# A two-layer graph network on one core: three weight masks and the low parts of x on VectorE in stage one, two more adjacency tiles split

## The reference

```python
node = x @ W1                                  # 4096 x 16
hw = einsum('nc,kcf->nkf', x, W2)              # 16 products of 128 x 128
x0 = einsum('nk,nkf->nf', node, hw)
x1 = layernorm(x + relu(adj @ x0 + node @ b0))

sens = exp(-(1/adj - 1)**2 / (2 * 0.5**2))
weights = where(adj < 1, sens, 0)              # 4096 x 4096
out = layernorm(x1 + weights @ (x1 @ W + B))
```

## Time and profile before

| | |
|---|---|
| median of 3 runs | 548.31 us (548.08 to 548.40) |
| the profiled execution: its time, its span | 548.46 us, 546.6 us |
| TensorE, VectorE, ScalarE, GpSimd busy | 99%, 92%, 91%, 15% of the span |
| granted TensorE clock | full in all slices but the last, 0.99 there |

### The profile page before, as it was taken

How to read it: one execution, slowest core, us unless ns; L and a number is a source line. 1 busy time by engine, 2 the same in 40 slices (tenths; PEclk the granted TensorE clock), 3 DMA queues, 4 the chain that set the end, 5 groups by cost and what they waited for, 6 DMA issues and landing times.

```text
span 546.6 us, 5236 instructions
## 1 busy us (share of the span) xinstructions
PE 541.2 (99%) x1800; PEld 332.0 (61%) x1800; DVE 504.6 (92%) x561; ACT 498.2 (91%) x449; POOL 83.3 (15%) x76
## 2 busy tenths in 40 slices
PE   9999999999999999999999999999999999999996
PEld 8888888655655565556555655565556556554444
DVE  5767777899999999999999999999999999999887
ACT  4778888669999999999999998999899899999994
POOL 1789989500000000000000000000000000000000
PEclk9999999999999999999999999999999999999999
DMA  5894000199998988888888898898988886870003
GB/s 165 321 424 173 27 2 0 31 367 422 414 360 300 339 335 315 303 330 314 334 306 314 321 349 305 312 317 320 327 315 308 316 330 236 322 267 1 0 19 135
DMA packets 23130, 142.05 MB, mean 260 GB/s; under 512 B 2720, under 2 KB 3264, under 8 KB 6720
## 3 DMA queue, kind: packets, MB, share of 16 engines
q1 hardware_dynamic: 22960, 141.46, 69.7%
q10 hardware_dynamic: 144, 0.26, 0.2%
HBM read 139.62 MB, written 2.10 MB: 259 GB/s over the span
## 4 chain that ended last, share of the span: by engine, by line
PE 99%; ACT 0%; DVE 0%; issue 0%; POOL 0%; ACTq 0%; POOLq 0%
PE kept_ps L526 20%; PE l_ps L526 18%; PE acc_ps L475 14%; PE acc_ps L464 7%; PE acc_ps L465 7%; PE acc_ps L466 7%; PE hw_ps L434 6%; PE hw_ps L440 5%; PE hw_ps L437 5%; PE acc_ps L526 2%; PE acc_ps L412 1%; PE var_ps L507 1%; PE acc_ps L481 1%; PE hw_ps L554 1%; PE acc_ps L536 0%; PE kept_ps L536 0%
## 5 line engine op out<-in xcount | busy, mean ns | idle before, releaser
L935 DVE SCALAR_TENSOR_TENSOR wt_pair<-wt_pair 128x2048 f32<-128x2048 f32 x60 | 136.9, 2283 | 1.3 <-DMA wt_pair<-adjT_dram 1.3
L642 ACT ACTIVATE wt_pair<-wt_pair 128x4096 f32<-128x4096 f32 (+1 forms) x33 | 108.9, 3300 | 11.7 <-DVE wt_pair L935 11.7
L647 ACT ACTIVATE wt_pair<-wt_pair 128x4096 f32<-128x4096 f32 (+1 forms) x33 | 109.1, 3307 | 0.5
L526 PE MATMUL kept_ps<-wt_pair,msg 128*128 128x512 f32 x240 | 107.9, 592 | 0.0
L923 DVE TENSOR_TENSOR row_lo<-rows,adj_hi 128x2048 fp32r<-128x2048 f32 x42 | 96.3, 2292 | 1.4
L526 PE MATMUL l_ps<-wt_pair,msg 128*128 128x512 f32 x216 | 97.1, 592 | 0.0
L626 ACT ACTIVATE prods<-hw_ps,node 128x128 f32<-128x128 f32 x256 | 73.1, 373 | 19.1 <-PE hw_ps L440 17.5
L890 DVE SCALAR_TENSOR_TENSOR part_acc<-hw_ps,node,part_acc 128x128 f32<-128x128 f32 x224 | 60.8, 343 | 20.7 <-PE hw_ps L440 20.7
L475 PE MATMUL acc_ps<-rows,x 128*128 128x512 f32 x176 | 78.8, 592 | 0.0
L464 PE MATMUL acc_ps<-adj_hi,x_hi 128*128 128x512 f32 x168 | 75.5, 449 | 0.0
L526 PEld LDWEIGHTS kept_ps<-wt_pair,msg 128*128 128x128 f32 x240 | 45.4, 190 | 49.3 <-issue 47.8
(11 more groups left out here) (122 smaller groups left out, 603.4 us busy)
## 6 DMA issues: line engine op xcount, KB each, us to landing
rows<-adjT_dram SPq DMA_DIRECT2D x68, 1024.0 KB, 4.9
wt_pair<-adjT_dram SPq DMA_DIRECT2D x60, 1024.0 KB, 4.8
x_in<-xT_dram SPq DMA_DIRECT2D x8, 256.0 KB, 3.6
x_row<-xT_dram SPq DMA_DIRECT2D x8, 256.0 KB, 5.1
outT_dram<-sumT SPq DMA_DIRECT2D x7, 256.0 KB, 2.0
W_in<-W_dram SPq DMA_DIRECT2D x3, 256.0 KB, 4.8
W_in<-W_dram ACTq DMA_DIRECT2D x1, 256.0 KB, 3.7
outT_dram<-sumT SPq DMA_DIRECT2D x2, 128.0 KB, 1.9
```

The lines of the kernel that those rows point to most:

```text
L526: mm = pe.matmul(out, msg[:, c % 2, k, :], wt[t][:, k, :], start=(first and k == 0), stop=(last and k == CH - 1))
L642: act.activation(w, w, ACT.Ln, bias=TINY).then_inc(ln_made, 1)
L647: act.activation(w, w, ACT.Exp, scale=-1.0).then_inc(inv_made, 1)
L935: dve.scalar_tensor_tensor(out=w, in0=w, scalar=1.0, in1=w, op0=ALU.is_lt, op1=ALU.mult).then_inc(made, 1)
```

## The change

- Row tiles 14 (row 1, block 6) and 62 (row 7, block 6) are split too; 44 tiles are now. Since no block is split in some early row and unsplit in the last ones any more, the low parts of x0 all lie in place of x0, the separate `x0_apart` is gone, and three remainders wait for the unsplit tiles of rows 0 and 1 to be done.
- In stage one the low part of the next block of x is made by VectorE, between its pairs 1 and 2, and no longer by GpSimd.
- The masks of weight tiles 0, 1 and 2 are made by VectorE in stage one, behind blocks 2, 4 and 6.
- The first six weight tiles are loaded ahead of the first five row tiles.
- The written-out orders of VectorE and ScalarE in stage two are new in many places; on ScalarE the rounding of the last block of x0 stands behind the first Ln and Exp of tile 0.

```diff
-SPLIT = (1, 3, 4, 5, 6, 7)
-SPLIT_FIRST = ((3, 5, 7), (1, 3, 5, 7))
...
+SPLIT_IN_ROW = ((3, 5, 7), (1, 3, 5, 6, 7)) + 6 * ((1, 3, 4, 5, 6, 7),)
...
+MASKS_AFTER = (2, 4, 6)
...
+            for t in range(WT_RING - LATE_SLOTS):
+                load_wt(t)
             for i in range(ROW_RING):
                 load_row_tile(i)
-            for t in range(WT_RING - LATE_SLOTS):
-                load_wt(t)
...
-            round_x0(NB - 1)
             take_ln(0)
             take_inverse(0)
+            round_x0(NB - 1)
             take_square(0)
...
+            def remainder_of_x(g):
+                s = g % 2
+                dve.wait_ge(x_hi_made, g + 1)
+                dve.tensor_tensor(x_lo[:, s, :], x_in[:, s, :], x_hi[:, s, :], ALU.subtract).then_inc(x_lo_made, 1)
 
             def sum_over_k(g):
                 s = g % 2
                 dve.wait_ge(node_copied, g + 1)
                 for q in range(QUARTERS):
+                    if q == QUARTERS // 2 and g + 1 < NB:
+                        remainder_of_x(g + 1)
                     dve.wait_ge(hw_made[0], g * GROUPS + 2 * q + 2)
...
+                if g not in LO_APART:
+
+                    at_least(dve, row_tile_done, max([i + 1 for i in range(g, TILES, NB) if not is_split(i)], default=0))
...
+                if g in MASKS_AFTER:
+                    mask(MASKS_AFTER.index(g))
...
-            def remainder_of_x(g):
-                s = g % 2
-                pool.wait_ge(x_hi_made, g + 1)
-                pool.tensor_tensor(x_lo[:, s, :], x_in[:, s, :], x_hi[:, s, :], ALU.subtract).then_inc(x_lo_made, 1)
...
             for g in range(NB):
-                if g + 1 < NB:
-                    remainder_of_x(g + 1)
                 fold(g)
```

More of the change, by code:

```diff
@@ L27 @@
 COL_LAG = 13
-SPLIT = (1, 3, 4, 5, 6, 7)
-SPLIT_FIRST = ((3, 5, 7), (1, 3, 5, 7))
-LO_APART = (1, 4, 6)
-SIXTH, SIXTH_ROWS = 6, (2, 3, 4, 5, 6)
-SPLIT_LAST = (1, 3, 4, 5, 7)
+SPLIT_IN_ROW = ((3, 5, 7), (1, 3, 5, 6, 7)) + 6 * ((1, 3, 4, 5, 6, 7),)
+SPLIT = tuple(sorted(set().union(*SPLIT_IN_ROW)))
+LO_APART = tuple(g for g in SPLIT if any(g in row and g not in SPLIT_IN_ROW[-1] for row in SPLIT_IN_ROW))
 FIRST_PAIR = 6
+MORE_ON_ACT = ()
 BY_TILE = 54
@@ L94, in is_split @@
     def is_split(i):
[L95 to L100, removed]
+        return i % NB in SPLIT_IN_ROW[i // NB]
     def on_dve(m):
         if in_pair(m):
-            return (m - FIRST_PAIR) % 4 >= 2 or m >= BY_TILE
+            return ((m - FIRST_PAIR) % 4 >= 2 and m not in MORE_ON_ACT) or m >= BY_TILE
         return False
@@ L726, in _ @@
             take_ln(8)
-            square(1)
             take_exp(6)
@@ L1106, in _ @@
             add_part(3)
+            take_square(8)
+            split_row_tile(20)
+            mask(13)
             round_square(1)
             remainder_of_square(1)
-            split_row_tile(20)
-            mask(13)
-            take_square(8)
             mask(14)
@@ L1114, in _ @@
             split_row_tile(21)
+            mask(15)
             scale_row(1)
-            mask(15)
             split_row_tile(22)
@@ L1125, in _ @@
             add_part(9)
+            mask(17)
+            residual(2)
+            mask(18)
+            round_row(2)
             split_row_tile(27)
-            residual(2)
-            mask(17)
-            round_row(2)
-            mask(18)
             remainder_of_row(2)
@@ L1159, in _ @@
             mask(27)
-            add_part(19)
-            mask(28)
             take_square(24)
             round_square(3)
+            mask(28)
+            remainder_of_square(3)
+            add_part(19)
+            mask(29)
             split_row_tile(36)
-            remainder_of_square(3)
-            mask(29)
             add_part(21)
@@ L1169, in _ @@
             split_row_tile(37)
+            scale_row(3)
             mask(31)
-            scale_row(3)
             split_row_tile(38)
+            add_part(23)
+            copy_messages(3)
             add_row(3)
-            copy_messages(3)
-            add_part(23)
+            take_square(28)
             mask(32)
             split_row_tile(39)
-            take_square(28)
+            mask(33)
+            add_part(25)
+            mask(34)
+            residual(4)
             split_row_tile(41)
-            add_part(25)
+            round_row(4)
             split_row_tile(43)
-            residual(4)
-            mask(33)
-            round_row(4)
-            mask(34)
             remainder_of_row(4)
@@ L1230, in _ @@
             copy_messages(5)
+            mask(48)
+            split_row_tile(55)
             take_square(44)
-            split_row_tile(55)
-            mask(48)
             split_row_tile(57)
             add_part(41)
-            split_row_tile(59)
-            residual(6)
-            mask(49)
-            round_row(6)
-            mask(50)
-            remainder_of_row(6)
-            mask(51)
+            mask(49)
+            residual(6)
+            mask(50)
+            round_row(6)
+            mask(51)
+            remainder_of_row(6)
+            split_row_tile(59)
             add_part(43)
@@ L1246, in _ @@
             split_row_tile(60)
-            mask(53)
             remainder_of_square(6)
             take_square(48)
+            mask(53)
             add_part(45)
```

230 lines of the change are left out of this document (114 added, 116 removed).

## The result

| | before | after |
|---|---|---|
| median, beside each other on one chip | 548.19 us (545.88 to 548.40) | 557.86 us (555.04 to 558.10) |
| ratio of the two | | 1.0184 (1.0153 to 1.0215) |
| profiled execution, its span | 548.46 us, 546.6 us | 558.10 us, 556.3 us |

A forecast was written before the change was run, and what follows sets the result against it. TensorE's own work, busy 99% of the span, was taken as the bound. The sum -1.4 + 0.9 + 0.5 + 1.2 = +1.2 us gave 549.5 us against the median, with a range from 546.8 to 556.0 us.

The forecast's parts named there:

- The three masks and seven low parts in stage one: Stage one, VectorE beside GpSimd: masks fit the spare time, low parts fit a gap between pairs; taken as nothing.
- Rival B: Stage one: GpSimd and VectorE hold each other up, 4 to 8 us together, 553 to 557 us; chance 0.26.
- First new wait: block 4 of x: Stage one: later low part delays block 3's load, so block 4 lands late; TensorE waits 0.9 us, bounds 0 to 1.35.
- Second: the messages of row 0: Column tile 0: tile 9's mask stands ahead of the message copy; TensorE waits 0.5 us, bounds 0 to 0.9.
- Third: the square of row 1: Row 1: VectorE work behind weight tile 12's landing makes the square late; TensorE waits 1.2 us, bounds 0 to 2.0.
- What two more split tiles give: TensorE's own work: each split tile saves 0.72 us, two of them give 1.4 us less.
- the lead that the early masks give cannot be kept: Stage two, VectorE: it already waits 1.3 us for weight tile 12, and whoever comes earlier waits longer.
- The spare half microsecond behind each mask: Stage one, block 3: pair 0 ends at 50.9, TensorE needs its banks at 51.4, so masks cost nothing.
- The swap of loads: Load queue: five row tiles and six weight tiles swapped all land long before 103 us; nothing.
- the order of `round_x0`: Last block of x0, rounded behind two ScalarE passes of tile 0: covered by the last fold and tile 3's split; nothing.
- the end of the kernel: Last stage: orders differ but the chain goes through the same products; taken as 0, with 0.3 us either way.
- rival E: End of the kernel: VectorE late after tile 62's split, TensorE waits up to 2 us more, 551.5 us; chance 0.07.

The follow-up runs named there:

- e4: Changed kernel with GpSimd's stage-one additions replaced by constant writes, half of the sums over k left out; 1.0015 of the kernel before.
- e10: Changed kernel with the load of block 4 of x queued ahead of the five row tiles; 1.0212 of the kernel before.
- e11: Changed kernel, low parts of x back on GpSimd, early masks replaced by one-input sums into a 128-column buffer; 1.0011 of the kernel before.
- e3: Kernel before with tiles 14 and 62 split in the old orders, stage one untouched; 1.0191 of the kernel before.
- e1: Kernel before with only the low parts of x moved to VectorE; 1.0084 of the kernel before.
- e5: Changed kernel with the three early masks replaced by sums with one SBUF input, weight tiles 0 to 2 unmasked; 1.0096 of the kernel before.
- e8: Changed kernel with the copy of row 0's messages ahead of the mask of tile 9; 1.0198 of the kernel before.

## Why the prediction was wrong, point by point

- **The step that failed is "The three masks and seven low parts in stage one"**: "I take nothing, since both engines' durations are steady in all other rows". What it put at nothing measured 9.7 us in stage one, 0.9 of which it had foreseen as the late block of x. The steady rows had no such pair in them: before the change VectorE's sums in stage one had one input in PSUM, and its work with two inputs in SBUF stood where GpSimd is idle, from 4.97 to 9.45 us (GpSimd idle from 2.2 to 11.16) and from 104.75 us on (GpSimd done at 104.3). Rival B named the mechanism and the place, and had the rule of the Trainium skill beside it; it deserved most of the chance, since a rule that says "these two exclude each other" was weighed against rows that could not speak on it.
- **Rival B's size was too small too** (4 to 8 us, measured 9.7). Masks: 3.3 to 5.7 foreseen, 4.6 alone. Low parts: 1 to 2 foreseen, 5.3 alone (the late block of x in it, which the forecast had apart with 0.9). That they would be held up for 2.1 us nearly every time, and leave 0.4 of it each, it had right. It left out that a late low part also holds back a load, and that a wait can bring the clock down.
- **"First new wait: block 4 of x"**, 0.9 us: the mechanism is right, and where the low part has its own length (e4) the wait is 0.9. In the changed kernel the low parts of blocks 1 and 2 end 2 us later still, and the load of block 3 goes out at 18.31 instead of the 16.2 foreseen; block 4, issued at 30.41, lands 20.2 us later:

```profile
30.41 20.17 DMA x_in<-xT_dram
50.60 0.63 ACT x_hi L602
51.23 1.04 ACT prods L623 x4
52.32 0.50 PE hw_ps L431
```

  (the chain that ended last, in order of time). TensorE waits 2.2 us there; but e10 shows that the mask alone would cost 1.8 of it.
- **"Second: the messages of row 0"**, 0.5 us, bounds 0 to 0.9: it came, with 1.1 at the weight load, or 0.9 by the start of the product, by which the prediction reckoned (161.20, with 9.7 of stage one, against 150.56). Weight tile 9 landed later than I had it, and the mask waited 2.84 us for it:

```profile
158.25 2.29 DVE L938 SCALAR_TENSOR_TENSOR wt_pair<-wt_pair 128x2048 f32<-128x2048 f32 x1 [2.84 <-DMA wt_pair<-adjT_dram]
160.46 0.68 DVE L992 TENSOR_TENSOR msg<-var_ps,small 128x512 f32<-128x512 f32 x1
```

- **"Third: the square of row 1"**, 1.2 us, bounds 0 to 2: in the changed kernel 0, since tile 12 came earlier against TensorE's work and its mask waited only 0.63 us. In e11 TensorE waited some 0.5 us at this place and in e10 some 1.4 with the same orders, so it is a wait at the edge, as the bounds said. Why the landing moves by 1 to 3 us from kernel to kernel was not tried.
- **"What two more split tiles give"**, 1.4 us: right, 0.69 and 0.70. Their VectorE work was hidden, as said, but only with the masks made early (e3 has neither room nor lead): "the lead that the early masks give cannot be kept" does not hold.
- **The spare half microsecond behind each mask** holds for the first two; behind the third, in block 7, even an undisturbed mask makes TensorE wait 0.8 us (e4, e11), a term that the sum lacks.
- **The swap of loads, the order of `round_x0`, the end of the kernel** (rival E): nothing, or 0.2 us. In e11, where all of them are in, no time is lost there.

Added up in the changed kernel: +9.7 - 1.4 + 1.1 + 0.2 = +9.6, and the profiled executions differ by 9.64. The run nearest to the forecast's own assumptions is e4, in which masks and low parts stay on VectorE and collide with nothing: by the distances it is 1.2 us longer than the kernel before, the forecast's number, at a ratio of 1.0015 (0.9997 to 1.0033). The number fits by luck in part: 0.9 for block 4 of x is right, but 0.8 behind the last mask and 0.4 more at the messages stand in the place of the 1.2 for the square.

## What to carry to other kernels

Before work is moved between VectorE and GpSimd, or into a stage where the other one works, ask of each instruction how many inputs it has in SBUF and whether GpSimd reads SBUF then; "idle beside it" is no cover if the two exclude each other. A duration that is steady in a profile says nothing on a pair that this profile never had side by side. And an idle engine's free time can be a lead that a later stage lives on: put the early work where it collides with nothing, or leave it out together with what it pays for.

## What the runs showed that I had not expected

- **A wait costs more than its length.** Behind TensorE's wait at the last mask the granted clock goes to half (1.2 of 2.4 GHz). Products of TensorE, and its windows, where the clock stands third from the end:

```profile
105.71 0.50 PE L431 MATMUL hw_ps<-W_hi,x_hi 128*128 128x512 f32 x1 [2.37 <-DVE part_acc L890]
106.04 0.53 PE L434 MATMUL hw_ps<-W_hi,x_lo 128*128 128x512 f32 x1
106.37 0.63 PE L437 MATMUL hw_ps<-W_lo,x_hi 128*128 128x512 f32 x1
...
106.00:110.00 4.00, 4.00 (x12) 3.10 (x12) 2.12 (x9) 1.14 (x4) 3.84 (x4) 0.57 0.01 4
110.00:113.00 3.00, 3.00 (x15) 2.47 (x14) 2.35 (x10) 2.42 (x9) 1.01 (x2) 1.00 0.00 0
```

  From 106.37 to 109.36 the products come every 427 ns instead of 227; the nine from 105.71 on take some 1.6 us more than they should, on top of a wait of 2.8. It fell so behind waits of 2.2 to 4.7 us in e1, e3, e5 and e8, and three times in e10 behind waits of 1.8, 1.8 and 2.8. Behind the changed kernel's own waits of 2.2 (52.32) and 1.8 (79.97) it did not, so the length of the wait alone does not settle it; what else does was not tried.
- **Two hundredths decide who waits.** With the low parts on VectorE the mask comes 0.4 to 0.5 us behind GpSimd's addition; without them it comes 0.02 us ahead. The same three masks last 4.1 us or 2.3 us, and the loss moves from VectorE's pairs to ScalarE's buffer.
- **Four bytes.** A buffer of 4 bytes in each partition, allocated ahead of others, made the float32r products of the split tiles come every 230 to 232 ns instead of 227 to 228: 1.2 us over the kernel (443.7 against 444.9 for the rest). The float32 products stayed at 429 ns.
